# A twelve-stage decoder kernel: rotary attention by a lane shuffle, constant products in TensorE's waits, and an earlier router load

## The reference

```python
x = x + L0_attn(layernorm(x)); x = x + L0_xattn(layernorm(x), ctx); x = x + L0_ffn(layernorm(x))
... # the same for L1, L2 and L3, each with its own kind of attention and of experts

def L2_attn(x, Wq, Wkv, Wo, bo):         # 16 heads of 64, 4 key heads
    q, k, v = heads(x @ Wq), heads(x @ Wkv[keys]), heads(x @ Wkv[values])
    q = q * cos + rotate_half(q) * sin   # rotate_half(x1, x2) = (-x2, x1), halves of 32
    k = k * cos + rotate_half(k) * sin
    return softmax(scale * q @ k.T) @ v @ Wo + bo
```

## Time and profile before

| | |
|---|---|
| three runs | 2924.52, 2919.11, 2916.24 us |
| median | 2919.11 us |
| the profiled execution | 2919.91 us |
| its span, first to last instruction | 2918.1 us |
| mean granted PE clock | 0.870 |
| busy: PE, PEld | 2344.6 (80%), 1534.3 (53%) us |
| busy: DVE, ACT, POOL | 1589.7 (54%), 1306.9 (45%), 751.3 (26%) us |
| L1a | 592.4 to 993.8 us of the span |
| L1f | 1327.2 to 1526.0 |
| L2a | 1535.2 to 1877.8 |

### The profile page before, as it was taken

The page is one execution under the profiler, slowest core; times in us unless marked ns, Lnnn a source line. Parts: engine busy times, 40 slices in busy tenths (PEclk is TensorE's granted clock), DMA queues, the critical chain, the costliest instruction groups (busy, mean ns, idle before and its releaser), DMA issues. The chain is left out here.

```text
span 2918.1 us, 49184 instructions
## 1 busy us (share of the span) xinstructions
PE 2344.6 (80%) x16209; PEld 1534.3 (53%) x16238; DVE 1589.7 (54%) x4946; ACT 1306.9 (45%) x3187; POOL 751.3 (26%) x1054
## 2 busy tenths in 40 slices
PE   6969895667887389883478999876969997899989
PEld 4624443644554234442366777555847775455553
DVE  4757773145556587762215555363447775777730
ACT  4715553124455135553424666532326654255442
POOL 0122211533232422200373333114621112222100
PEclk9969996858888578896688999997989998699989
DMA  2022225220000032213160000125420000322200
GB/s 74 2 75 85 81 66 153 51 72 15 30 30 15 27 87 78 78 38 101 50 124 12 2 1 2 44 68 141 146 86 1 2 2 21 92 73 75 63 17 15
DMA packets 131357, 160.30 MB, mean 55 GB/s; under 512 B 23171, under 2 KB 93452, under 8 KB 129957
## 3 DMA queue, kind: packets, MB, share of 16 engines
q1 hardware_dynamic: 115528, 132.84, 15.7%
q0 software_dynamic: 12976, 23.22, 3.0%
q10 hardware_dynamic: 2624, 1.32, 0.3%
HBM read 120.82 MB, written 37.79 MB: 54 GB/s over the span
## 5 line engine op out<-in xcount | busy, mean ns | idle before, releaser
L725 DVE CUSTOM_DVE_ANT_0 L3x_ps_ring<-L3x_ps_ring,L3x_mask_q 128x512 f32<-128x512 f32 x256 | 174.0, 709 | 68.0 <-PE L3x_ps_ring L960 53.5
L728 DVE TENSOR_REDUCE L0x_mx<-L0x_ps_ring 128x1 f32<-128x512 f32 x256 | 166.8, 686 | 70.7 <-PE L0x_ps_ring L960 69.9
L728 DVE TENSOR_REDUCE L1x_mx<-L1x_ps_ring 128x1 f32<-128x512 f32 x256 | 166.1, 686 | 61.9 <-PE L1x_ps_ring L960 61.0
L856 ACT ACTIVATE L3x_p_ring<-L3x_ps_t 128x1024 f32<-128x1024 f32 x128 | 131.1, 1025 | 146.0 <-PE L3x_ps_t L999 145.8
L856 ACT ACTIVATE L1x_p_ring<-L1x_ps_t 128x1024 f32<-128x1024 f32 x128 | 130.4, 1025 | 121.4 <-PE L1x_ps_t L992 120.7
L856 ACT ACTIVATE L0x_p_ring<-L0x_ps_t 128x1024 f32<-128x1024 f32 x128 | 130.4, 1025 | 105.6 <-PE L0x_ps_t L992 105.1
L1368 ACT ACTIVATE L2a_probs<-L2a_ps_s,L2a_top 128x256 f32<-128x256 f32 x256 | 118.0, 473 | 93.2 <-DVE L2a_top L1318 92.3
L992 PE MATMUL L3x_ps_t<-L3x_q_stack,L3x_k_stack 75*128 75x256 bf16 x512 | 124.6, 279 | 5.5 <-ACT L3x_p_ring L856 5.4
L960 PE MATMUL L1x_ps_ring<-L1x_k_stack,L1x_q_stack 72*128 72x512 bf16 x256 | 103.8, 430 | 30.3 <-DVE L1x_mx L728 16.4
L960 PE MATMUL L0x_ps_ring<-L0x_k_stack,L0x_q_stack 72*128 72x512 bf16 x256 | 103.1, 428 | 29.2 <-DVE L0x_mx L728 15.6
L999 PE MATMUL L3x_ps_t<-L3x_mask_k,const_ident_bf 128*128 128x256 bf16 x512 | 124.3, 279 | 0.0
(11 more groups left out here) (687 smaller groups left out, 6134.7 us busy)
## 6 DMA issues: line engine op xcount, KB each, us to landing
L0x_k_stack<-L0x_k_dram SPq DMA_DIRECT2D x96, 96.0 KB
L1x_k_stack<-L1x_k_dram SPq DMA_DIRECT2D x96, 96.0 KB
L3x_k_stack<-L3x_k_dram SPq DMA_DIRECT2D x96, 96.0 KB
L0f_w<-L0f_in_w SPq DMA_DIRECT2D x32, 256.0 KB, 7.9
L1a_rk_wide<-L1a_rk_dram SPq DMA_DIRECT2D x8, 1024.0 KB, 4.6
L1f_w<-L1f_in_w SPq DMA_DIRECT2D x32, 256.0 KB, 3.2
kept_x<-ctxT SPq DMA_DIRECT2D x24, 256.0 KB, 3.2
L0x_q_stack<-L0x_q_dram SPq DMA_DIRECT2D x96, 48.0 KB
```

The lines of the kernel that those rows point to most:

```text
L725: dve.tensor_tensor_reduce(bank, bank, mask_q[:, qt, :], 1.0, 2 * MASKED, ALU.add, ALU.max, accum_out=mx[:, qt, h:h + 1]).then_inc(took_se ...
L728: dve.tensor_reduce(mx[:, qt, h:h + 1], bank, AX, ALU.max).then_inc(took_sem(n), 1)
L856: act.activation(pr, pt, ACT.Exp, scale=scale).then_inc(exp_done.sem, 1)
```

## The change

**L2a.** The columns of every head's q and k weights are re-ordered on the host (`PAIRED`), so that the partner of each value in rotate_half lies 16 lanes away in the same group of 32. An item now holds two chunks of plain weights, so a batch has 4 q items and 1 k item, each with the same two products as before. DVE makes two multiplies of 128x512, first sin and then cos, into `tilted`; waits for the first; and exchanges its lanes with one STREAM_SHUFFLE of 128x512 into `swapped`. POOL adds the two in one 128x512 instruction. `scores` waits, unit by unit, only for the q and the k item that it reads; in the stages without rotation (L0a and L3a) the same code waits for the items' copies. `w_qr` and `w_kr` (0.65 MB) are no longer loaded.

**keep_clock** is `keep_busy` as a function of the module. It puts products of constants ahead of waits: 102 in the three cross-attentions, 8 in L2x, 120 in L0f, 50 in L1f, 62 in L2f, 20 in L3f, and 205 in L1a with its tail (29 at the start, 28 in the tail, and 148 in the loop: 42 before the first `dots`, 28 before the fourth, 18 before the k items, 20 in the last two batches' first `turn`, 40 before `y`), 567 in all. In L1a some also wait for a copy of a bank, since they write into it.

**L1f.** The two small loads are issued at the start of the norm's block, x is stored ahead of xn, the block no longer waits for the two stores, and POOL waits for them (`stored`, 32) before its gathers.

```diff
+def keep_clock(pe, const, bank, times):
+    wide = const["max_rows"][:, 0:4, :].rearrange("p a k -> p (a k)")
+    for _ in range(times):
+        pe.matmul(bank, const["ones_bf"][:], wide, start=True, stop=True)
...
 # attention_rows: POOL, DVE, PE
-                        wait_taken(pool, o)
-                        dst = qT[:, b % 2, k, :] if kind == "q" else kT[:, b % 2, k, :]
-                        part = turned[:, (rotation_count[o] - 1) % 3]
-                        pool.tensor_tensor(dst, part[:, 0, :], part[:, 1, :], ALU.add).then_inc(rotated, 1)
+                        r = rotation_count[o] - 1
+                        pool.wait_ge(swap_done, r + 1)
+                        dst = (qT if kind == "q" else kT)[:, b % 2, 2 * k:2 * k + 2, :]
+                        pool.tensor_tensor(dst.rearrange("p c s -> p (c s)"), tilted[:, r % 2, 0, :], swapped[:, r % 2, :],
+                                           ALU.add).then_inc(rotated, 1)
...
-                        if rotation_count[o] > 3:
-                            dve.wait_ge(rotated, rotation_count[o] - 3)
-                        dve.tensor_tensor(turned[:, (rotation_count[o] - 1) % 3], item_bank(o).rearrange("p (a s) -> p a s", a=2),
-                                          angles[kind][:], ALU.mult).then_inc(took["dve"], 1)
+                        r = rotation_count[o] - 1
+                        if r >= 2:
+                            dve.wait_ge(rotated, r - 1)
+                        halves = lambda a: a.rearrange("p (c s) -> p c s", c=2)
+                        for a in (1, 0):
+                            across = angles[kind][:, a:a + 1, :].broadcast_to([P, 2, S])
+                            last = dve.tensor_tensor(halves(tilted[:, r % 2, a, :]), halves(item_bank(o)), across, ALU.mult)
+                            last.then_inc(tilt_done if a else took["dve"], 1)
+                        dve.wait_ge(tilt_done, r + 1)
+                        dve.stream_shuffle(swapped[:, r % 2, :], tilted[:, r % 2, 1, :], [(i + 16) % 32 for i in range(32)]).then_inc(swap_done, 1)
...
-                        if k == 0:
-                            for what in ("q", "k"):
-                                wait_taken(pe, [i for i in items if i[0] == what and i[1] == b][-1])
+                        c = k * RS // R
+                        needed = [[i for i in items if i[:2] == (what, b) and 2 * i[2] <= last][-1]
+                                  for what, last in (("q", c), ("k", cfg["kchunk"](c)))]
+                        for i in needed:
                             if rope:
-                                pe.wait_ge(rotated, max(rotation_count[i] for i in rotations if i[1] == b))
+                                pe.wait_ge(rotated, rotation_count[i])
+                            else:
+                                wait_taken(pe, i)
...
 # attention_fidelity, PE
+                idle_at_first = {("x", 0, 0): 12, ("q", 0, 0): 2, ("k", 0, 0): 2, ("c", 0, 0): 3, ("x", 1, 0): 7, ("rows", 0, 0): 3}
...
+                    if kind == "dots" and k == 0 and b >= 1:
+                        wait_copied(pe, (b - 1) * H + 4)
+                        keep_clock(pe, const, ps_p[:, ((b - 1) * H + 4) % 2, :], 6)
+                    if kind == "dots" and k == 3 and b >= 1:
+                        wait_copied(pe, (b - 1) * H + 6)
+                        keep_clock(pe, const, ps_p[:, ((b - 1) * H + 6) % 2, :], 4)
...
-                            keep_busy(pe, ps_p[:, n % 2, :], 2)
+                            keep_clock(pe, const, ps_p[:, n % 2, :], 12 if b >= B - 2 and h == 0 else 2)
...
 # ffn_choosing_experts
-        normalize_all(nc, x_sb, xn, xT, const, cfg["name"] + "ln_", [("xn", xn_dram), ("x", sum_dram[0])])
+        loaded, temp_in, stored = sem("loaded"), sem("temp_in"), sem("stored")
+        normalize_all(nc, x_sb, xn, xT, const, cfg["name"] + "ln_", [("x", sum_dram[0]), ("xn", xn_dram)], stored,
+                      [(w_r[:], w["w_r"], loaded), (temp[:, 0:1], w["log_temp"].broadcast_to([P, 1]), temp_in)])
...
 # L2a's slots
-   slots=[([("x",0,1)],[("k",0,1)]),([("q",0,1)],[("k",1,1)]),([("q",1,1)],[("y",0,-1)]),([("q",2,1)],[("v",0,1)]),
-          ([("q",3,1)],[("y",1,-1)]),([("q",4,1)],[("q",5,1)]),([("q",6,1)],[("ln",0,2)]),([("q",7,1)],[("ln_rest",0,2)])]),
+   slots=[([("x",0,1)],[]),([("k",0,1)],[]),([("q",0,1)],[("y",0,-1)]),([],[("v",0,1)]),
+          ([("q",1,1)],[("y",1,-1)]),([("q",2,1)],[]),([],[("ln",0,2)]),([("q",3,1)],[("ln_rest",0,2)])]),
```

More of the change, by code:

```diff
@@ L140, in plan_rows @@
     if cfg.get("rope"):
-        a.take("w_kr", [nkc * P])
         a.take("angles_k", [2, S])
-        a.take("w_qr", [cfg["chunks"] * P])
         a.take("angles_q", [2, S])
@@ L878, in step @@
                         if kind == "x":
+                            if isinstance(b, int) and b == 0:
+                                keep_clock(pe, const, bank, 10)
                             wait_step(pe, ln_done, b, 3 * QT + 1)
@@ L1178, in attention_rows @@
         took = {"act": sem("act_took"), "dve": sem("dve_took")}
-        rotated = sem("rotated")
+        rotated, tilt_done, swap_done = sem("rotated"), sem("tilt_done"), sem("swap_done")
         s_full, top_done, exp_done = sem("s_full"), sem("top_done"), sem("exp_done")
@@ L1790, in _ @@
             def _(sp):
-                sem.start(sp)
-                if to_dram is not None:
-                    for what, dst in to_dram:
-                        if what == "xn":
-                            sp.wait_ge(normed, NT)
-                        s = xn if what == "xn" else x_sb
-                        sp.dma_start(dst.rearrange("(t p) d -> p t d", p=P), s[:]).then_inc(stored, 16)
-                    sp.wait_ge(stored, 16 * len(to_dram))
+                for dst, s, landed in loads:
+                    sp.dma_start(dst, s).then_inc(landed, 16)
+                for what, dst in to_dram:
+                    if what == "xn":
+                        sp.wait_ge(normed, NT)
+                    s = xn if what == "xn" else x_sb
+                    sp.dma_start(dst.rearrange("(t p) d -> p t d", p=P), s[:]).then_inc(stored, 16)
         sem.clear()
@@ L3146, in wait_wide_read @@
                 eng.wait_ge(qc_out, b + 1)
-        def keep_busy(pe, bank, times):
-            for _ in range(times):
-                pe.matmul(bank, const["ones_bf"][:], const["max_rows"][:, 0:4, :].rearrange("p a k -> p (a k)"), start=True, stop=True)
         with nc.Block() as block:
@@ L3429, in _ @@
                     par, g = b % 2, b * GROUPS + k
+                    if o in idle_at_first:
+                        keep_clock(pe, const, ps_p[:, 1, :], idle_at_first[o])
+                    if kind == "dots" and k == 0 and b >= 1:
[4 more added lines that the diff above has]
+                        keep_clock(pe, const, ps_p[:, ((b - 1) * H + 6) % 2, :], 4)
+                    if kind == "k" and b >= 2:
+                        wait_copied(pe, (b - 2) * H)
+                        keep_clock(pe, const, ps_p[:, (b - 2) * H % 2, :], 3)
                     if o in number:
@@ L3866, in consts @@
     return c
+PAIRED=[d+e for d in (0,16) for h in (0,32) for e in range(h,h+16)]
 def rope_table():
```

43 lines of the change are left out of this document (26 added, 17 removed).

## The result

The changed kernel took 2846.75 us in the median of four runs (2843.97 to 2849.15), the kernel before, run beside it, 2917.68 (2912.14 to 2924.52). The ratio is 0.9755 with a 95% interval of 0.9731 to 0.978: 71 us less. The forecast was 2836, its range 2804 to 2872. In the profiled executions the span went from 2918.1 to 2847.3 us and the granted clock from 0.870 to 0.905.

What follows compares the result with a forecast made beforehand. It took PE to bound L2a, PE's clock L1a, and a wait for stores and the router's load L1f's start. Terms -32, -28, -5, -2, -8.8, -1.5, -6 took 2919.9 to 2836.6, less 0.8: 2836 us, range 2804 to 2872.

Steps and rivals of the forecast that it cites:

- the other starts: Products of constants at the starts of L0f, L2f, L3f, L2x and the cross-attentions: -6 us together, between -14 and +20.
- L2a, -32: L2a's projections: five rotated items a batch instead of ten, 0.92 us of PE each, over seven batches; -20 to -38.
- all of it on the path as long as PE stays the bound: In L2a's loop: the 32 us of projections leaving PE shorten the stage in full while PE is its bound.
- the 3 us given back for lateness: At L2a's first scores: later rotation and POOL's larger add cost 3 us, offsetting 3 saved by fewer items.
- Rival 2: In L2a DVE is late, so PE waits 0.5 us in five units of eight batches: 2856 us, chance 0.12.
- L1a, -35: Products of constants keep PE's clock full in L1a: -28 us in the loop, -5 at the start, -2 in the tail.
- my two bounds: Per slow stretch of L1a's loop: 4.6 us shorter from PE alone, 2.8 if PE kept its 74% share; 4.0 taken.
- Rival 1: In L1a the clock drops as before, so its 35 us go: 2871 us, or 2853 with half; chance 0.17.
- L1f, -10.3: L1f: -8.8 us from earlier loads and no wait for stores, -1.5 from products ahead of the first expert.
- Rivals 3, 4 and 5: Rival 3 below; 4: no clock rise, half of L2a, 2894 to 2914, 0.03; 5: denser PE gets low clock, 2962, 0.04.
- rival 3: PE is not L2a's bound, so fewer projections there change nothing: 2868 us, chance 0.04.

Runs made afterwards that it cites:

- e4: The full change with L2a's norm of the next batch but one placed one unit earlier; 2904.56 us on a slower chip, ratio 0.9758 to the kernel before.
- e5: The full change with L2a's last q item in the seventh unit and the norm's last step alone in the eighth; 2840.56 us, ratio 0.9722.
- e9: The full change with another table placing L2a's items and norm steps in the units; 2897.37 us on a slower chip, ratio 0.9767.
- e7: The full change without the 362 products of constants outside L1a; 2851.35 us, ratio 0.9756.
- e2: The kernel before with only the products of constants in L1a and its tail added; 2930.96 us on a slower chip, ratio 0.9856.
- e8: The full change without the loop products in L1a ahead of the fourth dots, the k item and y; 2863.11 us, ratio 0.9799.
- e11: The full change without the 34 products of constants in each of the three cross-attentions; 2904.76 us on a slower chip, ratio 0.9801.

## Why the prediction was right, and where it was off

**What binds, and the sum.** Right: L2a was bound by PE, L1a by PE's clock, L1f's start by the stores. The sum is partly luck. L2a gave 14.2 us less than foretold and the other starts 7.8 less; L1a gave 8.8 more and L1f 0.5, so that of 22.0 us missed only 12.7 show.

**L2a, -32; measured -17.8.** This is the step that failed. Its price of an item, 0.92 us, was nearly right: without its wait the period would be 37.60 - 1.61 = 35.99, so five items are worth 4.25 us, 0.85 each. The step "all of it on the path as long as PE stays the bound" and the 3 us given back for lateness were wrong: PE did not stay the bound in every unit, and 14.8 us came back as waits of PE for the norm, where 3 had been set off. The prediction's own sign of being wrong, that PE in L2a shows waits for DVE or POOL, came true for this stage. In the trace 15.6 us came after the stage's first maxima and 2.2 ahead of them (3 in the text): the first scores start 6.0 us sooner, but DVE turns the other q items first, and its maxima come 5.9 us behind the scores where it was 2.1. Rival 2 had the direction, a DVE late in a unit; it gave 20 us back where 14.2 were missing, and its cause, a slow shuffle, was wrong. The shuffle took 0.73 us, the forecast 0.69. I had counted DVE's time per unit and taken the norm's step at its mean; I had not asked what POOL's longer add would hold. That this one hold is the whole cause is not shown: e4 and e5 took the wait away and the period fell by 0.1 us. POOL's add was bounded with 0.73 and 1.46 and took 1.28. e9 shows that most of the -32 was to be had with another table: 343.5 - 315.6 = 27.9. Of the wrong step, then, the runs show that where the items stand decides it, and leave open which of the moves does.

**L1a, -35; measured -43.8.** The slow stretches went, and each was worth 4.6 us (period 40.87 to 36.06 is 4.8), the upper one of my two bounds, and not 4.0: PE alone set their length, as the busy shares of DVE and ACT there had said. That makes 32 for 28. The start gave 10 for 5: the window now has clock 0.78. Some 3 to 5 of these 10 are owed to products ahead of the stage (e7, e2), which the prediction had not counted. The tail gave 1.4 for 2. Rival 1 fell, but e8 shows how near it was: with 86 of the loop's 148 added products gone, 18 of the 44 us go, though the longest wait keeps its six.

**L1f, -10.3; measured -10.8.** The logits start 10.0 us sooner (8.8 foretold), their own clock gives 1.5 more, the burst ahead of the first expert -1.2 (-1.5 foretold); 2 us are given back at the stage's end, where DVE waits longer for the sums.

**The other starts, -6; measured +1.8.** L2x and L3f gave 6, the cross-attentions took 5.7, which e11 shows to be chance. In L0f the burst ended 7 us too early, in L2f also; the sentence that PE often idles again behind such a burst was the right one, and the -1 that I still gave L2f was not.

**The granted clock** could be trusted: where it went from 0.50 to 1.00, `dots` went from 2.08 to 1.13 us, and the stage became 44 us shorter. The caution in the Trainium skill, "TensorE: Matmul & The Clock Gate", Part 1, does not show here.

**Rivals 3, 4 and 5** fell. By rival 3 fewer projections would have given nothing; they gave 17.8 us, and 27.9 with the better table. The Trainium skill, "Perfetto Trace Analysis", Identifying the Most-Contended Engine, which stood beside it, calls matmul busy time no good measure of how close PE is to its peak. That is another question than the one here, which engine sets the pace of a loop: there PE's records left no gap, 200.00 of 200 us, and the lines of DVE waited for it.

## What to carry to other kernels

Before moving work from a full engine to one with room, write down what each of its instructions will stand in front of, on every queue that it touches: with DVE at an average load of 68%, DVE and POOL were late at one or two points of the batch, and the table of items that put them there cost a third of what the stage could gain (17.8 of 27.9 us came). When a wait that you name goes and the period stays, look for its successor before you look for the next cause. Products of constants ahead of the longest wait of a round alone did not hold the clock here; with the shorter waits filled too it held (e8). A burst gave a loop a start at full clock where it ended about as the loop began (L1f with 1.12 us between and L3f), and not where PE idled 6.98 us behind it (L0f).
